# Two passes or three for the rotated query of a cross-attention block

## The reference, cut to what matters

```
q_hk  = (layernorm(x) @ Wq.T)                     # per head 128 columns
q_big = apply_rope(einsum('bshk,hkq->bshq', q_hk, w_kc_q))   # 384 columns
q_r   = einsum('bshq,hqr->bhsr', q_big, W_qr)     # 64 columns
k_r   = einsum('bld,hdr->bhlr', kv_r, W_kr)       # 64 columns
attn  = softmax(einsum('bhsr,bhlr->bhsl', q_r, k_r))
ctx   = einsum('bhsl,bld->bhsd', attn, kv_r)      # then w_kc_kv and Wo
x = x + ctx_lat @ Wo.T
x = x + ffn(layernorm(x))
```

## Time and profile before

| | |
|---|---|
| median of 3 runs | 860.63 us (858.93 to 863.16) |
| span of the profiled execution, first to last instruction | 861.5 us |
| time of the profiled execution outside its span | not shown |
| PE busy, matmuls | 757.3 us (88%), 3268 |
| DVE busy, operations | 766.2 us (89%), 1026 |
| ACT busy | 573.6 us (67%) |
| POOL busy | 577.6 us (67%) |

### The profile page before, as it was taken

How to read it: one execution, slowest core, us unless ns; L and a number is a source line. 1 busy time by engine, 2 the same in 40 slices (tenths; PEclk the granted TensorE clock), 3 DMA queues, 4 the chain that set the end, 5 groups by cost and what they waited for, 6 DMA issues and landing times.

```text
span 861.5 us, 12578 instructions
## 1 busy us (share of the span) xinstructions
PE 757.3 (88%) x3268; PEld 487.1 (57%) x3268; DVE 766.2 (89%) x1026; ACT 573.6 (67%) x838; POOL 577.6 (67%) x581
## 2 busy tenths in 40 slices
PE   3678998989999999999999999999999675868996
PEld 3555565756666666666566656665666442424543
DVE  5799899989998999899989999999999767797895
ACT  2477677767766867687667766776777576774332
POOL 5769674867486757766776668576848474867462
PEclk9889999999999999999999999999999797889999
DMA  9216867776768576858676766677668999400000
GB/s 330 79 49 115 169 130 140 138 167 134 151 114 170 117 161 132 170 111 167 118 160 134 152 128 138 149 137 150 125 146 213 241 227 275 164 0 25 13 24 37
DMA packets 294405, 118.50 MB, mean 138 GB/s; under 512 B 271856, under 2 KB 278000, under 8 KB 294128
## 3 DMA queue, kind: packets, MB, share of 16 engines
q1 hardware_dynamic: 293568, 116.68, 62.0%
q10 hardware_dynamic: 816, 1.57, 0.5%
HBM read 49.02 MB, written 2.10 MB: 59 GB/s over the span
## 4 chain that ended last, share of the span: by engine, by line
PE 35%; POOL 20%; DVE 18%; issue 11%; DMA 7%; SPq 5%; ACT 3%; POOLq 1%; DVEq 0%; ACTq 0%
PE banks L1419 22%; POOL rot_cos L1055 5%; PE scores L1720 5%; DMA load<-in_pack 4%; POOL rot_lo L1063 4%; SPq L943 4%; PE scores L1507 3%; PE banks L1735 3%; DVE neg_max L1323 3%; POOL rot_hi L1061 2%; DVE rows L1330 2%; POOL rot_sin L1046 2%; DVE rot_cos L1295 2%; DVE cv_lo L1288 1%; POOL wq_lo L388 1%
## 5 line engine op out<-in xcount | busy, mean ns | idle before, releaser
L1185 ACT ACTIVATE scores<-scores,neg_max 128x1024 f32<-128x1024 f32 x128 | 139.2, 1087 | 56.1 <-DVE neg_max L1323 54.6
L1330 DVE SCALAR_TENSOR_TENSOR rows<-scores,rows 128x1024 f16<-128x1024 f32 x128 | 154.9, 1220 | 13.7 <-ACT rows L1196 12.6
L1419 PE MATMUL banks<-pt,v_hi 128*128 128x512 f16 x512 | 154.3, 383 | 12.5 <-DMA pt<-rows 11.4
L1323 DVE TENSOR_REDUCE neg_max<-scores 128x1 f32<-128x1024 f32 x128 | 155.5, 1216 | 2.9 <-PE scores L1507 2.7
L1055 POOL TENSOR_TENSOR rot_cos<-rot_cos,rot_sin 128x512 f32<-128x512 f32 x93 | 119.2, 1281 | 46.6 <-DVE rot_sin L1297 42.2
L1196 ACT ACTIVATE rows<-scores 128x1024 f16<-128x1024 f32 x128 | 130.8, 1022 | 5.2
L1063 POOL TENSOR_TENSOR rot_lo<-rot_cos,rot_hi 128x512 fp32r<-128x512 f32 x93 | 119.6, 1286 | 7.8
L1159 ACT CAST cv_hi<-banks 128x512 fp32r<-128x512 f32 x64 | 37.6, 587 | 102.6 <-PE banks L1419 101.4
L1318 DVE SCALAR_TENSOR_TENSOR acc<-banks,inv,acc 128x512 f32<-128x512 f32 x128 | 91.4, 745 | 8.0 <-PE banks L1419 4.1
L1419 PE MATMUL banks<-pt,v_lo 128*128 128x512 f16 x256 | 97.8, 382 | 0.0
L1419 PEld LDWEIGHTS banks<-pt,v_hi 128*128 128x128 f16 x512 | 44.5, 98 | 79.2 <-issue 36.4
(11 more groups left out here) (211 smaller groups left out, 1824.7 us busy)
## 6 DMA issues: line engine op xcount, KB each, us to landing
load<-in_pack SPq DMA_DIRECT2D x15, 320.0 KB, 3.5
raw_chunk<-in_out_w SPq DMA_DIRECT2D x8, 512.0 KB, 5.2
raw_chunk<-in_gate_w SPq DMA_DIRECT2D x8, 512.0 KB, 4.4
raw_chunk<-in_val_w SPq DMA_DIRECT2D x8, 512.0 KB, 4.6
raw<-in_gate_w SPq DMA_DIRECT2D x8, 512.0 KB, 5.5
raw<-in_val_w SPq DMA_DIRECT2D x8, 512.0 KB, 5.2
raw<-in_out_w SPq DMA_DIRECT2D x8, 512.0 KB, 7.0
load<-in_pack SPq DMA_DIRECT2D x15, 256.0 KB, 3.3
```

The lines of the kernel that those rows point to most:

```text
L1185: nc.scalar.activation(scores[:, u % 2, :], scores[:, u % 2, :], ACT.Exp, bias=neg_max[:, u:u + 1], accum_out=sums[:, u:u + 1]).then_inc(e ...
L1323: nc.vector.tensor_reduce(neg_max[:, u:u + 1], scores[:, u % 2, :], AX, ALU.max, negate=True).then_inc(max_ready, 1)
L1330: nc.vector.scalar_tensor_tensor(out=rows[:, u % ROWS, 1, :], in0=scores[:, u % 2, :], scalar=WEIGHT_LIFT, in1=rows[:, u % ROWS, 0, :], op ...
L1419: mm = nc.tensor.matmul(out, ws[a], xs[c], start=first and n == 0, stop=last and n == 2)
```

## The change

`wr` holds the high columns twice side by side, and the low columns twice side by side, as two stationary operands of 128 columns. Each chunk of `C` takes three passes instead of two. The whole product then stands in both halves of the bank, ACT takes the high part out with one copy on 128 partitions, and DVE the low part with one subtraction. The `double` items, `rest`, `rest_ready` and `doubled` go. The scores wait for `group_read` of `C` in their place. POOL's split of `wr` writes each part twice. To make room, `ident_b` moves into memory that is free after the heads, and its cast goes from the end of the heads into the feed-forward's first tile.

```diff
     def rotated(h, src):
-        split(h, 2, [t["wr"][:, :, half, :] for half in range(2)],
-              src[:, 0:CQ * R].rearrange("p (c r) -> p c r", c=CQ)).then_inc(wr_ready, 1)
+        wr, plain = t["wr"], src[:, 0:CQ * R].rearrange("p (c r) -> p c r", c=CQ)
+        for twin in range(2):
+            ins = nc.gpsimd.tensor_scalar(wr[:, :, 0, twin, :], plain, 1.0, 0.0, ALU.mult, ALU.add)
+        ins.then_inc(t["split_hi"], 1)
+        pool.wait_ge(t["split_hi"], h.after(5, 3))
+        for twin in range(2):
+            ins = nc.gpsimd.tensor_tensor(wr[:, :, 1, twin, :], plain, wr[:, :, 0, twin, :].bitcast(F32), ALU.subtract)
+        ins.then_inc(wr_ready, 1)
...
                 elif kind == "C":
-                    src = banks[0:R, p.bank[marked], :]
-                    nc.scalar.copy(qr[0][0:R, group[1], :], src)
-                    out = qr[0][R:2 * R, group[1], :]
+                    out = qr[0][:, group[1], :]
...
-            def double(p, marked):
-                b = marked[1]
-                done = p.earlier(("C", b, "next")) if marked[-1] == "last" else p.place(("C", *marked[1:]))
-                act.wait_ge(group_read, p.read(done))
-                nc.scalar.copy(qr[1][0:R, b, :], qr[1][R:2 * R, b, :]).then_inc(doubled, 1)
...
                     if kind == "C":
-                        b, low = group[1], slice(R, 2 * R)
-                        nc.vector.tensor_tensor(rest[low, b, :], banks[0:R, bank, :], qr[0][0:R, b, :].bitcast(F32),
-                                                ALU.subtract).then_inc(rest_ready, 1)
-                        dve.wait_ge(rest_ready, h.after(B, b + 1))
-                        return nc.vector.tensor_tensor(qr[1][low, b, :], banks[low, bank, :], rest[low, b, :], ALU.add)
+                        pair = [x[:, group[1], :] for x in qr]
...
-                        for half in range(2):
-                            mm = nc.tensor.matmul(out, wr[:, c].rearrange("p o r -> p (o r)"), rot[half][:, c, :],
-                                                  start=c + half == 0, stop=c + half == CQ)
+                        mm = three(out, [wr[:, c, half].rearrange("p o r -> p (o r)") for half in range(2)],
+                                   [x[:, c, :] for x in rot], c == 0, c == CQ - 1)
...
+                places = [p.place(("C", b)) if p.first else p.earlier(("C", b, "next"))]
                 if not odd:
                     here = b or p.first
-                    pe.wait_ge(group_read, p.read(*(p.place(("K", b, half)) if here else p.earlier(("K", 0, half, "next"))
-                                                    for half in range(2))))
-                pe.wait_ge(doubled, p.head.after(B, b + 1))
+                    places += [p.place(("K", b, half)) if here else p.earlier(("K", 0, half, "next")) for half in range(2)]
+                pe.wait_ge(group_read, p.read(*places))
...
-            nc.gpsimd.tensor_copy(t["ident_b"][:], t["ident"][:]).then_inc(t["constants"], 1)
...
                 pool.wait_ge(out_bias_loaded, 16)
+                nc.gpsimd.tensor_copy(t["ident_b"][:], t["ident"][:])
...
-            t["wr"] = early.enter_context(nc.sbuf_tensor("wr", [P, CQ, 2, R], F32R, side="right"))
+            t["wr"] = early.enter_context(nc.sbuf_tensor("wr", [P, CQ, 2, 2, R], F32R, side="right"))
```

More of the change, by code:

```diff
@@ L74 @@
 A0, A1, V1, V0, C0, C1 = ("A", 0, "next"), ("A", 1, "next"), ("V", 1, "last"), ("V", 0), ("C", 0, "next"), ("C", 1, "next")
-UNGROUPED = ("score", "max", "exp", "sum", "double", "abs", "drop", "stats", "spread", "root", "deviation", "norm", "extreme", "scale", "X", "take", "first root",
+UNGROUPED = ("score", "max", "exp", "sum", "abs", "drop", "stats", "spread", "root", "deviation", "norm", "extreme", "scale", "X", "take", "first root",
              "turn", "start root", "values", "count", "variance", "inverse", "normed", "rotate", "products", "rotated",
@@ L102 @@
     ("high", 7, "last"), ("K", 1, 0), A0, ("K", 1, 1), ("exp", 0), ("high", 0), ("exp", 1), ("high", 1),
-    ("B", 0, 2, "next"), V1, ("exp", 2), ("high", 2), ("exp", 3), ("double", 1, "last"), ("high", 3), A1, ("abs", 2),
-    ("M",), ("exp", 4), ("high", 4), C0, ("exp", 5), ("high", 5), ("B", 1, 2, "next"), ("double", 0, "next"), V0,
+    ("B", 0, 2, "next"), V1, ("exp", 2), ("high", 2), ("exp", 3), ("high", 3), A1, ("abs", 2),
+    ("M",), ("exp", 4), ("high", 4), C0, ("exp", 5), ("high", 5), ("B", 1, 2, "next"), V0,
     ("exp", 6), ("high", 6), ("exp", 7), C1,
@@ L108 @@
     ("high", 7, "last"), A0, ("exp", 0), ("high", 0), ("exp", 1), ("high", 1), ("B", 0, 2, "next"), V1, ("exp", 2),
-    ("high", 2), ("exp", 3), ("high", 3), ("double", 1, "last"), A1, ("M",), ("abs", 0), ("exp", 4), C0, ("high", 4),
-    ("exp", 5), ("high", 5), ("K", 0, 0, "next"), ("K", 0, 1, "next"), ("B", 1, 2, "next"), V0, ("double", 0, "next"),
+    ("high", 2), ("exp", 3), ("high", 3), A1, ("M",), ("abs", 0), ("exp", 4), C0, ("high", 4),
+    ("exp", 5), ("high", 5), ("K", 0, 0, "next"), ("K", 0, 1, "next"), ("B", 1, 2, "next"), V0,
     ("exp", 6), ("high", 6), ("abs", 1), ("exp", 7), C1,
@@ L143 @@
     ("turn", "x", 4), ("turn", "x", 5), ("turn", "k", 1), ("abs", 2), ("rotate", 0, 0), ("rotate", 0, 1),
-    ("rotate", 0, 2), ("A", 1), ("abs", 0), ("C", 0), ("turn", "k", 0), ("double", 0), ("abs", 1), ("spread most",),
-    A0, ("K", 0, 0), ("K", 0, 1), ("Y", 3), ("values", 0), ("values", 1), ("C", 1), ("exp", 0), ("double", 1),
+    ("rotate", 0, 2), ("A", 1), ("abs", 0), ("C", 0), ("turn", "k", 0), ("abs", 1), ("spread most",),
+    A0, ("K", 0, 0), ("K", 0, 1), ("Y", 3), ("values", 0), ("values", 1), ("C", 1), ("exp", 0),
     ("high", 0), ("exp", 1), ("high", 1), ("Y", 2), ("K", 1, 1), ("M",), ("B", 0, 2, "next"), ("exp", 2), ("high", 2),
     ("K", 1, 0), ("exp", 3), ("high", 3), A1, ("exp", 4), ("high", 4), C0, ("exp", 5), ("high", 5),
-    ("B", 1, 2, "next"), ("double", 0, "next"), V0, ("exp", 6), ("high", 6), ("exp", 7), C1,
+    ("B", 1, 2, "next"), V0, ("exp", 6), ("high", 6), ("exp", 7), C1,
 )
@@ L171 @@
     ("high", 7, "last"), ("exp", 0), ("high", 0), ("exp", 1), ("high", 1), ("exp", 2), ("drop", 0), ("high", 2), V1,
-    ("double", 1, "last"), ("exp", 3), ("high", 3), ("exp", 4), ("high", 4), ("drop", 1), ("exp", 5), ("high", 5),
+    ("exp", 3), ("high", 3), ("exp", 4), ("high", 4), ("drop", 1), ("exp", 5), ("high", 5),
     ("drop", 2), ("exp", 6), ("drop", 3), ("M",), ("high", 6), V0, ("exp", 7), ("first root",), ("high", 7),
@@ L804, in attention_heads @@
         qr = [placed(f"qr_{x}", [P, B, S], F32R) for x in ("hi", "lo")]
-        rest = nc.alloc_sbuf_tensor_at("rest", [P, B, S], F32, offset=at["qr_lo"])
         kr = [placed(f"kr_{x}", [P, B, L], F32R) for x in ("even", "odd")]
@@ L832, in attention_heads @@
         wq_ready, wc_ready, wr_ready, wk_ready, wv_ready, wo_ready = t["ready"]
-        rest_ready, doubled = sem("rest_ready"), sem("doubled")
         rot_sum, rot_hi, rot_ready = sem("rot_sum"), sem("rot_hi"), sem("rot_ready")
@@ L1209, in period @@
                         start.spread_most(act)
-                    elif item[0] == "double":
-                        double(p, item)
                     elif item[0] == "abs":
@@ L1266, in take_out @@
                     if kind == "C":
-                        b, low = group[1], slice(R, 2 * R)
-                        nc.vector.tensor_tensor(rest[low, b, :], banks[0:R, bank, :], qr[0][0:R, b, :].bitcast(F32),
-                                                ALU.subtract).then_inc(rest_ready, 1)
-                        dve.wait_ge(rest_ready, h.after(B, b + 1))
-                        return nc.vector.tensor_tensor(qr[1][low, b, :], banks[low, bank, :], rest[low, b, :], ALU.add)
-                    if kind == "K":
+                        pair = [x[:, group[1], :] for x in qr]
+                    elif kind == "K":
                         (up, into_up), (down, into_down) = keys_at(group)
@@ L1278, in take_out @@
                                                        ALU.subtract)
-                    if kind == "A":
+                    elif kind == "A":
                         pair = [x[:] for x in q]
@@ L1657, in feed_forward @@
     HC = HID // P
-    small = itertools.count(at["kr_odd"] + 4 * D, 32)
+    small = itertools.count(at["kr_odd"] + 4 * D + 2 * P, 32)
     def over(name, shape, place, dt=F32):
@@ L1663, in feed_forward @@
     t["out_b"] = over("out_bias", [P, D], at["kr_odd"])
+    t["ident_b"] = over("ident_b16", [P, P], at["kr_odd"] + 4 * D, BF16)
     gate, val, sigma = (over(n, [P, HID], at[place]) for n, place in (("gate", "v_hi"), ("val", "v_lo"), ("sigma", "probs")))
@@ L1980, in sb @@
             return ctx.enter_context(nc.sbuf_tensor(name, shape, dt))
-        t = {"acc": sb("acc", [P, NU, D]), "ident": sb("ident", [P, P]), "ident_b": sb("ident_b16", [P, P], BF16),
-             "ones": sb("ones", [P, P]), "partial": sb("partial", [P, 3 * CHUNKS]), "partial3": sb("partial3", [P, 3]),
```

(1 more changed line is left out.)

## The result

The changed kernel takes 864.3 us (median of 14 runs, 860.11 to 867.36) against 860.25 (14 runs, 857.47 to 863.66): a ratio of 1.0037, 95% interval 1.0020 to 1.0055. A second series gave 865.23 and 1.0053 (1.0036 to 1.0070). The change makes the kernel slower: the medians differ by 4.1 and 4.4 us, and the intervals go from +1.7 to +4.7 and from +3.1 to +6.0 us. At 0.4 to 0.5% that is about as much as I had said a measurement can tell. The forecast was +6.3 us.

A forecast was written before the change was run, and what follows sets the result against it. A loop of waits, not one engine's sum, was taken to set each pair of heads. +1.18 a pair gave +8.3 over seven pairs; with -0.9 and -1.1 at the ends, +6.3, so 866.9 us, range 863 to 871.

The forecast's parts named there:

- the last head's -1.1: From `C 1` to the max at 676.78: -0.59 for ACT's second copy, -0.72 for DVE, +0.23 for the third matmul.
- The signs named for a right forecast: Pairs of 84.2 to 84.8 us, DVE waiting some 0.5 ahead of `B 1 0`, POOL's wait for `B 1 1` growing, others shrinking.
- Odd head, +0.30 and +0.23: +0.30: late `B 1 0` and `B 1 1` delay score 5 and ACT's row 5; +0.23: `C 1`'s third part behind `rot_lo`.
- Even head, "+0.65": At `C 0`, `B 1 1` is taken 0.65 later, delaying POOL's rotations and the split of `wq`: +0.65 a pair.
- over DVE's `C 0`: Even head's other, nearly equal branch, with row transposes behind `C 0`: gains 0.72 and falls behind POOL's.
- Opening, -0.9: First head, PE's wait until 57.66 for `qr_lo` of `C 1`: 0.72 less, and some 0.2 of `C 0`'s earlier saving.
- POOL at nothing: Second copy and subtraction of `wr`, 0.94 a head, hidden behind POOL's waits; at most 6.6 in all if uncovered.
- matmuls at 0.228: Each of the 96 new `C` matmuls on PE costs 0.228: 21.9 us in all, 2.74 a pair.
- Here the saving is lost: Even head's `C 0`: DVE's branch gains 0.72, but POOL's branch decides, so the saving does not count.
- PE as the bound: Rival: all 96 new matmuls lie on the path, +21.9, 882 us; chance 0.07.
- DVE's relief: Rival: DVE's saving decides at the even head's `C 0`, -0.5 a pair, 855 us, at most 838; chance 0.14.
- Lost and won back: Rival: a shorter wait behind the last `C 1` keeps PE's clock up, 863 us, no measurable change; chance 0.26.

The follow-up runs named there:

- the relief by itself: The changed kernel with two passes a chunk of `C`, the pass with the low weights left out: 854.29 us, ratio 0.9923 to the kernel before.
- the kernel before with `B` earlier: PE's order in the kernel before turned to `C 0` part 0, `B 1 0`, part 1, `B 1 1`, part 2: 858.17 us, ratio 0.9977.

## Why the prediction was right or wrong

The direction was right, the size too large: +4.1 by the traces instead of +6.3. From the `M` of head 1 to that of head 14, 549.71 against 543.37 (means of two and of three traces), +6.3; opening -1.3; from there to the last `M`, 52.90 against 53.81, -0.9, with 1.4 between traces of one kernel. That makes +4.1, inside the intervals of both series (+1.7 to +4.7 and +3.1 to +6.0 us). The same stretches had +7.6 (seven odd, six even), -0.9 and -0.45 (the seventh even head's +0.65 and the last head's -1.1) in the forecast. Of the missing 2.2, 1.3 lie in the loop (0.6 in the odd heads, 0.7 in the even ones), where traces of one kernel differ by at most 0.6; the rest is no larger than such differences. The signs named for a right forecast all came (84.3 a pair, DVE's 0.55 ahead of `B 1 0`, POOL's longer wait for `B 1 1`), but none of them tells the two branches of the even head apart.

- **Odd head, +0.30 and +0.23:** right in mechanism, 0.53 against 0.45 measured. DVE waits for PE at `B 1 0`, its saving is half lost on ACT's row 5, PE's wait for `rot_lo` ahead of `C 1`'s last part is all but gone. The experiments add that `B 1 0` and `B 1 1` were only half the cause: with both at their old time 0.26 came back, and the rest only with score 5 ahead of the third part and ACT's copy turned.
- **Even head, "+0.65": the step that failed,** in its path more than in its size (0.53 by the means of 40.63 and 40.10). The forecast let POOL's branch alone carry the loss. By itself that branch costs 0.28 (40.34 against 40.06): the 0.16 ahead of the split of `wq`, which I took "for a mere hand-over and not for slack", was a wait for that split's own load, so rotations that end 0.77 later (16.47 behind the `M` instead of 15.70) start the split only 0.57 later (16.44 instead of 15.87). I counted only one other branch, "over DVE's `C 0`", and that one does fall behind: the load of `wq` at its end lands 15.50 behind the `M`, ahead of the rotations. The branch that I left out is PE's: its plain sum to the end of `V 0`, max 6, row 6 and SP's transpose lead to the load of `wc`, and cost 0.66 by themselves (40.70 against 40.04). I had followed DVE's saving and not PE's passes beyond score 5, and had not seen that SP's list puts the load behind row 6's transpose; in the kernel before, too, it lands 0.71 behind that transpose (20.71 and 20.00 after the `M`; all these times are medians of six heads). That the size came out near is luck: three matmuls were priced at 0.65 on one path and cost 0.66 on another.
- **Opening, -0.9:** measured -1.3, partly at another clock; whether for the reason given is open.
- **POOL at nothing, matmuls at 0.228:** right. That passes and relief can be priced apart and added holds for the whole time within wide intervals, not by stretch: "Here the saving is lost" is true of `C 0` in the even head, but the saving makes up there for `C 1`'s passes, a cost of 0.27 that the forecast did not have.
- **Rivals.** PE as the bound is right in one place, from `C 0` to `V 0` in the even head, and wrong as a sum (1.74 of 2.74 a pair). DVE's relief does not decide. The Trainium skill's rule for the most contended engine (Perfetto Trace Analysis, Identifying the Most-Contended Engine) is borne out only for the relief by itself: DVE, first at 89%, worked less and 6.6 us came off. Exchanged for passes on PE, the engine with 57% by its weight loads, it lost. Lost and won back came near in time, not in mechanism: the slow stretch ahead of the last `M` is still there, from 687 on:

```profile
687.00:693.00 6.00, 4.58 (x10) 2.61 (x11) 3.62 (x5) 3.55 (x6) 4.42 (x3) 0.51 1.12 244
```

Of the versions tried that compute the whole product, only the kernel before with `B` earlier is measurably faster than the kernel before, by 0.23% and barely clear of noise; no version with three passes beats it.

## What to carry to other kernels

Before you price work added to an engine, find every branch that joins the critical one at the next meeting point (here a single load) and follow the added work along each; the chain of waits names only the one that ended last. Undoing a branch that is not the last shows nothing, and undoing the last one shows only the way to the next, so an experiment that moves nothing does not clear its suspect until the other branch is shortened too. An engine at 86 to 89% can be relieved by 25 us and give back 6.6.

## What was unexpected in the hardware

Three traces of one kernel differ by 5.2 us in the stretch behind the last `M`, and the shortest has the highest granted clock (0.98, against 0.93 in the window above and 0.92 in the third trace), so single traces say little about that stretch. The loop's stretches, at full clock, repeat within some 0.1 us in the median. And the order of SP's list reaches PE both ways: the load of `wc`, issued behind a transpose, landed 0.71 us after it in the kernel before and 0.78 in the changed one (medians), and with the load issued first, SP was busy with the two transposes until 5.20 us after it had begun them, and PE waited 1.00 for their rows.
